# Rounding a quantised layer's weight inside the attention before it, and three tails rearranged in an eight-layer fused kernel

## The reference

```python
x = x + L0_xattn(ln(x), ctx)      # 32 heads of 16, 8 key/value heads
x = x + L0_ffn(ln(x))             # 1792 hidden rows, the winner of each block of 32
x = x + L1_xattn(ln(x), ctx)      # 16 heads of 96, keys from ctx and x
x = x + L1_ffn(ln(x))             # Hadamard rotation, W, bias, LoRA
x = x + L2_xattn(ln(x), ctx)      # 32 heads of 128, 8 key/value heads, normed q and k, mask
x = x + L2_ffn(ln(x))             # fp8: one scale for all of x, one for the weight
x = x + L3_xattn(ln(x), ctx)      # autocorrelation by FFT, top 9 lags, softmax over them
x = x + L3_ffn(ln(x))             # w1, w3, w2 packed as int4 with a scale per group of 64
```

## Time and profile before

| | us |
|---|---|
| median of 3 runs (lowest, highest) | 1610.83 (1609.64, 1613.52) |
| the profiled execution | 1609.08 |
| its span | 1607.4 |
| PE busy | 1400.4 (87%) |
| DVE busy | 1098.7 (68%) |
| ACT busy | 728.5 (45%) |
| POOL busy | 689.5 (43%) |
| mean granted clock of PE | 0.943 of full speed |

### The profile page before, as it was taken

One profiled execution on the slowest core, in us unless ns is written; L12 is line 12 of the kernel. 1 busy time (PEld: TensorE's weight loads), 2 busy tenths in 40 slices (PEclk: granted clock), 3 DMA queues, 4 the chain that ended last, 5 costly groups with the idle time before them and its releaser, 6 DMA issues. The chain is left out here.

```text
span 1607.4 us, 31525 instructions
## 1 busy us (share of the span) xinstructions
PE 1400.4 (87%) x11376; PEld 838.9 (52%) x11376; DVE 1098.7 (68%) x2220; ACT 728.5 (45%) x2379; POOL 689.5 (43%) x662
## 2 busy tenths in 40 slices
PE   5888499986999998669999999999995848659997
PEld 4775244445777776236555655555552325224443
DVE  7997565536657667668878878878776879765212
ACT  4775363213433332228666666666551426354110
POOL 4887441004433334306656666666652025543000
PEclk9998699997999999779999999999998769979998
DMA  7999371109999889346545545665334102276001
GB/s 192 184 172 181 87 158 38 22 6 186 177 181 169 145 136 140 90 124 135 123 109 127 114 113 114 117 138 103 73 76 124 42 0 37 46 155 100 5 1 52
DMA packets 515369, 172.50 MB, mean 107 GB/s; under 512 B 473761, under 2 KB 498657, under 8 KB 515089
## 3 DMA queue, kind: packets, MB, share of 16 engines
q1 hardware_dynamic: 515216, 170.51, 53.6%
HBM read 53.27 MB, written 2.10 MB: 34 GB/s over the span
## 5 line engine op out<-in xcount | busy, mean ns | idle before, releaser
L1714 POOL TENSOR_TENSOR a_q_ss<-a_q_ss,half 128x4 f32<-128x4 f32 x64 | 89.2, 1394 | 188.9 <-DVE a_q_ss L1644 94.9
L1574 ACT ACTIVATE a_probs<-a_masked,a_negmax 128x128 f32<-128x128 f32 x256 | 99.6, 390 | 95.5 <-DVE a_negmax L1619 95.5
L67 PE MATMUL bank<-a_wq_hi,xn_pair 128*128 128x512 f16 (+1 forms) x384 | 139.0, 362 | 0.5 <-DVE a_qn L1649 0.5
L68 PE MATMUL bank<-a_wq_lo,xn_pair 128*128 128x512 f16 (+1 forms) x384 | 138.9, 362 | 0.0
L69 PE MATMUL bank<-a_wq_hi,xn_pair 128*128 128x512 f16 (+1 forms) x384 | 138.7, 361 | 0.0
L1159 POOL TENSOR_TENSOR a_p_hl<-a_probs,a_p_hl 128x512 f16<-128x512 f32 x64 | 74.1, 1158 | 150.0 <-DVE a_p_hl L1097 150.0
L67 PE MATMUL bank<-a_wo_hi,a_o_hi 128*128 128x512 f16 x256 | 97.0, 379 | 6.7 <-DVE x_state L1635 6.7
L69 PE MATMUL bank<-a_wo_hi,a_o_lo 128*128 128x512 f16 x256 | 97.0, 379 | 0.0
L68 PE MATMUL bank<-a_wo_lo,a_o_hi 128*128 128x512 f16 x256 | 97.0, 379 | 0.0
L1616 DVE TENSOR_TENSOR a_masked<-bank,a_mask 128x512 f32<-128x512 f32 x64 | 44.1, 689 | 71.6 <-PE bank L69 71.5
L1729 POOL TENSOR_TENSOR a_normal<-a_probs,a_recip 128x512 f32<-128x512 f32 x64 | 89.8, 1404 | 5.0
(11 more groups left out here) (400 smaller groups left out, 4990.7 us busy)
## 6 DMA issues: line engine op xcount, KB each, us to landing
a_no<-in_L_xattn_Wo SPq DMA_DIRECT2D x9, 1024.0 KB, 5.5
a_nq<-in_L_xattn_Wq SPq DMA_DIRECT2D x8, 1024.0 KB, 5.6
a_n_wq<-in_L_xattn_Wq SPq DMA_DIRECT2D x4, 768.0 KB, 6.6
a_n_wo<-in_L_xattn_Wo SPq DMA_DIRECT2D x4, 768.0 KB, 5.9
a_nk<-in_L_xattn_Wk SPq DMA_DIRECT2D x9, 256.0 KB, 3.1
a_nv<-in_L_xattn_Wv SPq DMA_DIRECT2D x9, 256.0 KB, 2.9
x_state<-in_x SPq DMA_DIRECT2D x8, 256.0 KB, 4.8
a_ctx<-in_ctx_t SPq DMA_DIRECT2D x8, 256.0 KB, 4.0
```

The costliest lines, as they stand in the source:

```text
L67: pe.matmul(out, lh, rh, start=start, stop=False)
L68: pe.matmul(out, lh, rl, start=False, stop=False)
L1574: m = act.activation(probs[s % 2][:, h, :], src, ACT.Exp, bias=negmax[s % 2][:, h:h + 1], accum_out=total[s % 2][:, h:h + 1])
L1714: pool.tensor_tensor(r[:, :], r[:, :], K.half[:, 0:n], ALU.pow).then_inc(root_done.sem, 1)
```

## The change

It has five parts.

1. First attention: ahead items 10 and 11 move from steps 68 and 69 to 75 and 76, behind the last heads; the small weights of stage 1 are loaded at step 50 and split earlier; its first large weights are loaded at step 78, and stage 1, not the end of this one, waits for them.
2. Wide attention: a new class `Quantised` holds the quantised layer's tensors. The weight is loaded at step 6 into half of `xn_rows`, its maximum taken in steps 12 to 15, made common on POOL in step 17, the scale computed in step 18, and the weight rounded in 20 steps of one DVE operation each (20 to 39); ACT casts it in step 61. ctx for the spectra is loaded at step 61. In the tail x of batches 0 to 6 is normalised and its maximum taken, a batch a step.
3. Quantised stage: only batch 7 is normalised; ACT takes the first step of each row's rounding; the 24 spectra are six before the rows and two or three for each batch between them; loops are written out. The packed words of the last layer's tile 0 are loaded here.
4. Lag attention: the ninth largest by one reduction; the sum of weights from the nine values alone; products with a broadcast operand; tile 0 of w1 and w3 is unpacked as chunks 11 and 12; statistics and roots of batches 0 to 3 for the last stage.
5. Last stage: tile 0 needs only its transposes, rows have four buffers, and each batch of x is stored after its own add.

```diff
-    LOAD_FRONT, MEAN_FRONT, CLEAR_FRONT, HIGH_FRONT, LOW_FRONT = TOTAL + 1, TOTAL + 1, TOTAL + 6, TOTAL + 8, TOTAL + 10
-    AHEAD = {B + i: TOTAL + 2 + i for i in range(front.AHEAD)}
+    LOAD_SMALL, MEAN_FRONT, CLEAR_FRONT, HIGH_FRONT, LOW_FRONT, LOAD_FIRST = TOTAL - 14, TOTAL + 1, TOTAL + 2, TOTAL + 3, TOTAL + 10, TOTAL + 14
+    AHEAD = {B: TOTAL + 2, B + 1: TOTAL + 3, B + 2: TOTAL + 11, B + 3: TOTAL + 12}
...
-                    if t == LOAD_FRONT:
-                        front.load(sp, front_small_in, front_first_in)
+                    if t == LOAD_SMALL:
+                        front.load_small(sp, front_small_in)
+                    if t == LOAD_FIRST:
+                        front.load_first(sp)
-                sp.wait_ge(front_first_in, 32)
...
+        self.nw = K.xn_rows[:, KT:2 * KT, :]
+        self.tw, self.te = K.xn_rows[:, 0, :], K.xn_rows[:, 1, :].bitcast(I32)
+        self.wq = K.ctx_hi[:, :, 0:DIM].bitcast(BF16)
...
+        LOAD, LARGEST, SHARED, SCALES, ROUND, CAST, CONTEXT, ROWS = 6, 12, 17, 18, 20, TOTAL - 3, TOTAL - 3, TOTAL - B + ADD
...
+                    if s == LOAD:
+                        sp.wait_ge(norm.ring.filled(B - 1), norm.ring.n_filled(B - 1))
+                        quant.load_weight(sp, quant_in)
+                    if s == CONTEXT:
+                        last = q_last(G - 1)
+                        sp.wait_ge(ring.filled(last), ring.n_filled(last))
+                        quant.load_context(sp, context_in)
+                sp.wait_ge(context_in, 32)
+                    if s == CAST:
+                        for last in (kv_last("k", G - 1), kv_last("v", G - 1)):
+                            act.wait_ge(ring.filled(last), ring.n_filled(last))
+                        act.wait_ge(chain, 1 + 4 + 5 * KT)
+                        act.activation(quant.wq, quant.nw, ACT.Copy).then_inc(cast_done, 1)
...
+                    if part == 0:
+                        link(dve.tensor_scalar(tw, w, quant.scale[:, 0:1], quant.FP8_MAX, ALU.mult, ALU.min))
+                    else:
+                        link(dve.tensor_tensor(w, tw, bits, ALU.subtract))
...
+                    if s == LARGEST:
+                        dve.wait_ge(quant_in, 16)
+                    if LARGEST <= s < LARGEST + KT:
+                        k = s - LARGEST
+                        m = dve.tensor_reduce(quant.weight_max[:, k:k + 1], quant.nw[:, k, :], AX.X, ALU.max, apply_absolute_value=True)
+                    if s == SCALES:
+                        dve.wait_ge(shared_done, 1)
+                        quant.scales(dve, 0, link)
+                    if ROUND <= s < ROUND + 5 * KT:
+                        round_weight(*divmod(s - ROUND, 5))
+                def row_ahead(b):
+                    dve.wait_ge(row_root, 2 * b + 2)
+                    if b == 0:
+                        dve.wait_ge(cast_done, 1)
+                    dve.tensor_scalar(K.xn_rows[:, b, :], K.x[:, b, :], quant.mv[:, b, 0:1], quant.rstd[:, b:b + 1],
+                                      ALU.subtract, ALU.mult).then_inc(row_xn, 1)
+                    dve.wait_ge(row_xn, b + 1)
+                    dve.tensor_reduce(quant.row_max[:, b:b + 1], K.xn_rows[:, b, :], AX.X, ALU.max, apply_absolute_value=True)
...
-                        K.take_stats(dve, b)
+                        r = K.take_stats(dve, b)
+                        if b < quant.ahead:
+                            link(r)
+                            dve.bn_aggr(quant.mv[:, b, :], K.stats[:, b, :]).then_inc(row_mean, 1)
...
+                def row_root_of(b):
+                    pool.wait_ge(row_mean, b + 1)
+                    pool.tensor_scalar(quant.rstd[:, b:b + 1], quant.mv[:, b:b + 1, 1], EPS, None, ALU.add).then_inc(row_root, 1)
+                    pool.wait_ge(row_root, 2 * b + 1)
+                    pool.tensor_tensor(quant.rstd[:, b:b + 1], quant.rstd[:, b:b + 1], K.half[:, 0:1], ALU.pow).then_inc(row_root, 1)
...
+                    if s == SHARED:
+                        pool.wait_ge(largest_done, 1)
+                        pool.partition_all_reduce(quant.whole[:, 0:1], quant.big[:, 0:1], P, bass.bass_isa.ReduceOp.max).then_inc(shared_done, 1)
+                    if 0 <= s - ROWS < quant.ahead:
+                        row_root_of(s - ROWS)
...
+            if q == 0:
+                engine.wait_ge(front.first_in, 32)
...
+    EARLY = 6
+    LATER = {i: list(range(EARLY + 3 * i, EARLY + 3 * i + 3)) if i < 2 else list(range(EARLY + 2 + 2 * i, EARLY + 4 + 2 * i)) for i in range(B)}
...
-                sp.dma_start(nw[:, :, :], weight.rearrange("(k p) n -> p k n", p=P)).then_inc(inw, 16)
                 packed.load_down(sp, words_here)
-                sp.wait_ge(words_here, 32)
+                packed.load_first(sp, words_here)
...
+                def round_fp8(b):
+                    dve.wait_ge(scaled_done.sem, scaled_done.count(b))
+                    link(dve.tensor_scalar(e[:, :], w[:, :].bitcast(I32), 0x7F800000, None, ALU.bitwise_and))
+                    link(dve.tensor_scalar(bits, bits, 2.0 ** -6, Q.MAGIC, ALU.max, ALU.mult))
+                    link(dve.scalar_tensor_tensor(w[:, :], w[:, :], -Q.FP8_MAX, bits, ALU.max, ALU.add))
+                    if b >= 2:
+                        dve.wait_ge(t_bank.filled(b - 2), t_bank.n_filled(b - 2))
+                    dve.scalar_tensor_tensor(xq[b % 2][:, :], w[:, :], Q.TOP, bits, ALU.min, ALU.subtract).then_inc(q_done.sem, 1)
...
+                dve.bn_aggr(Q.mv[:, LAST, :], K.stats[:, LAST, :]).then_inc(row_mean, 1)
+                dve.wait_ge(row_root, 2)
+                link(dve.tensor_scalar(xn[:, LAST, :], K.x[:, LAST, :], Q.mv[:, LAST, 0:1], Q.rstd[:, LAST:B], ALU.subtract, ALU.mult))
+                link(dve.tensor_reduce(Q.row_max[:, LAST:B], xn[:, LAST, :], AX.X, ALU.max, apply_absolute_value=True))
+                dve.tensor_reduce(Q.big[:, 1:2], Q.row_max[:, :], AX.X, ALU.max).then_inc(largest_done, 1)
                 dve.wait_ge(whole_done, 1)
...
+                Q.scales(dve, 1, link)
+                dve.sem_inc(scale_done, 1)
+                link(dve.tensor_tensor(Q.out_by[:, :], Q.back[:, 0:1], Q.back[:, 1:2], ALU.mult))
+                for b in batches:
+                    round_fp8(b)
+                    if b >= 2:
+                        add(b - 2)
+                add(B - 2)
+                add(B - 1)
...
-                spectra.multiply(pe)
+                spectra.begin(pe)
+                for u in range(EARLY):
+                    spectra.multiply(pe, u)
                 pe.wait_ge(const_done, 2)
...
+                    for u in LATER[b][0:1]:
+                        spectra.multiply(pe, u)
...
+                    for u in LATER[b][1:]:
+                        spectra.multiply(pe, u)
...
-                spectra.copy(act)
+                def scale(b):
+                    if b >= 3:
+                        act.wait_ge(q_done.sem, q_done.count(b - 3))
+                    act.activation(tw[b % 3][:, :], xn[:, b, :], ACT.Copy, scale=Q.scale[:, 1:2]).then_inc(scaled_done.sem, 1)
+                for u in range(EARLY):
+                    spectra.copy(act, u)
+                act.wait_ge(scale_done, 1)
+                for b in range(2):
+                    scale(b)
...
+                    if b + 2 < B:
+                        scale(b + 2)
+                    for u in LATER[b]:
+                        spectra.copy(act, u)
...
-        UNPACK = {-2: (0, 1, 2), -1: (3, 4, 5, 6), 0: (7, 8), 1: (9, 10)}
+        UNPACK = {-2: (0, 1, 2), -1: (3, 4, 5, 6), 0: (7, 8), 1: (9, 10), B: (11, 12)}
...
-                            act.wait_ge(own.sem, own.count("total", l))
+                            act.wait_ge(own.sem, own.count("left8", l))
+                    if m is not None:
+                        act.wait_ge(own.sem, own.count("beyond", m))
+                        act.activation(nine_e[:, :, :], beyond[:, :, :], ACT.Exp).then_inc(nine_done.sem, 1)
...
-                        for k in range(KT):
-                            i = dve.max(next8[:, k, :], left8[:, k, :])
-                        i.then_inc(own.sem, 1)
+                        dve.tensor_reduce(next8[:, :, 0], left8[:, :, :], AX.X, ALU.max).then_inc(own.sem, 1)
-                        dve.memset(next8[:, :, 1:8], GONE).then_inc(own.sem, 1)
-                        dve.wait_ge(own.sem, own.count("alone", m))
-                        dve.memset(spacer[:, :], 0.0)
+                        if m:
+                            dve.wait_ge(nine_done.sem, nine_done.count("x", m - 1))
+                        dve.tensor_tensor(beyond[:, :, :], nine[:, :, 0:9], nine[:, :, 0:1].broadcast_to([P, KT, 9]),
+                                          ALU.subtract).then_inc(own.sem, 1)
...
-                        dve.wait_ge(own.sem, own.count("picked", m))
-                        dve.tensor_reduce(total[:, :], picked[:, :, :], AX.X, ALU.add).then_inc(own.sem, 1)
```

(71 more changed lines are left out.)

337 lines of the change are left out of this document (191 added, 146 removed).

## The result

The changed kernel takes 1590.32 us (median of 4 runs, 1587.60 to 1594.24) against 1610.24 of the kernel before (median of 4): a ratio of 0.9875, 95% interval 0.9849 to 0.9900. That is 20 us faster where 38 were forecast, and 2.3 us above the upper end of the range (1560 to 1588). The profiled execution's span is 1588.7 us against 1607.4, so 18.7 of the difference can be followed in the traces.

A forecast was written before the change was run, and what follows sets the result against it. PE was taken to bound the wide attention, DVE the lag attention, with the quantised stage poorly overlapped. Terms -9.6 + 2.0 + 2.0 - 14.5 - 4.3 - 8.0 - 5.6 = -38.0 us gave 1573 us from 1610.83; range 1560 to 1588.

The forecast's parts named there:

- The sum's largest term: Quantised stage: work leaves the path to the first row and PE sets the loop; 14.5 us gained, range 8 to 18.
- Rival (2): Quantised loop: PE stays at the low clock, +21 us, 1594; 8%.
- The all-reduce: Wide attention, step 17: POOL's stall of 5.6 us behind the call costs PE 2.0 us; bounds nothing and 8.
- Rival (1): Step 17: the code load is paid before the all-reduce too, 6 us more POOL stall, +6, 1579; 12%.
- The lag attention: Lag attention: DVE's step 0.94 us shorter, less the added work; 4.3 us gained, range 2 to 6.
- small subtraction: Lag attention step: one reduction of 0.69 us and this subtraction replace four maxima, memset and gaps, saving 0.25 us.
- The last stage's start: Last stage: PE starts at about 10.9 us, second tile at 21.5; 8 us gained, range 5 to 10.5.
- The first attention's tail: End of first attention: last heads cast straight behind the mix; 9.6 us gained, between 5 and 12.
- Rival (3): First attention's tail: the last heads don't come earlier, only the forecast's 9.6 us goes, 1583; 12%.
- The wide attention's tail: Steps 61 to 68: the ACT cast and DVE's rows ahead cost 2.0 us, range 1 to 5.
- Stores: End of kernel: the last 256 KB goes out right behind its add; 5.6 us gained, range 5 to 6.5.
- Rival (5): Wide attention: DVE's added step makes it late for PE in each of 28 steps, +56 us, 1629; 3%.

The follow-up runs named there:

- e14: Changed kernel with the rows of all eight batches normalised at the head of the quantised stage, none in the wide attention's tail: 1585.92 us (0.9862).
- e1: Changed kernel with the all-reduce of the wide attention's step 17 replaced by a POOL copy of 128 x 1 values: 1582.07 us (0.9829).
- e5: Changed kernel with chunks 11 and 12 unpacked in step 2 of the lag attention instead of step 8: 1586.67 us (0.9857).
- e9: Changed kernel with stage 1's first large weights loaded four steps earlier, at step 74: 1588.94 us (0.9863).
- e10: Changed kernel with ahead items 10 and 11 back at steps 68 and 69, loads as changed: 1592.13 us (0.9887).
- e13: Changed kernel with all four loads for stage 1 back at step 65, ahead items 10 and 11 still behind the last heads: 1588.46 us (0.9883).

## Why the prediction was wrong, point by point

**The sum's largest term held.** The quantised stage gave 14.5 of 14.5. Its working (six spectra and their copies, then ACT's scaling and DVE's steps, 16.9 us to the first row; 3.1 a batch, PE in front) was met within 0.3 us and in its order: the copies ended 13.4 us into the stage, forecast 13.9. Rival (2), the low clock, did not come: transposes take 0.39 in the loop (its sum is 48.4 us and not 48.6, which changes nothing). The cover of 9 us for the all-reduce held too, with half a microsecond to spare, against a stall that the forecast didn't have; that was luck. What was wrong is that rows made in the tail were counted among what the head gains. With the copies in front they gave it nothing (e14), and the tail paid for them.

**The all-reduce (+9.6 instead of +2.0)** is the term that sank the forecast. The step that failed is the use of the earlier trace rows: the call begins 0.23 us after its input "since POOL had been idle 12.26 us", and from this I charged step 17 with the stall behind the call alone, though POOL has no such idle time there. The stall on the way in runs from the end of POOL's last ordinary operation, whether the input is there or not: 5.6 to 6.0 us in the twelve traces with a call in the wide attention, 8.8 to 9.8 in the quantised stage behind such a call, 6.75 without one (e1). In e14 the call is prompt behind 8.33 us of idle time, and in the earlier trace rows behind 12.26. That row could not tell "no stall" from "a stall that is hidden". The stall behind the call was short as well, 7.68 against 5.6. In the earlier trace rows the 5.6 are what is left behind the root's input; from the first DVE operation of the lag attention to the root it is 7.1 us there, and 6.9 in the changed kernel. With both stalls the root of step 18 is 11.5 us late, where I had 5.6. And the forecast had no term for the clock: of the 9.6 us PE stood idle for 7.75 and lost the other 1.9 at 1.2 GHz behind it. The range's upper bound for the term, 8, was 1.6 too low.
Rival (1) was this case at 12%, with a price of 6 on top of the 2.0: right in its mechanism, and 1.6 short, since the stall behind the call and the clock were not in it. The Trainium skill's rule (GPSIMD Engine Reference, 2.1 Instruction dispatch: about 6 us before the first call to a freshly loaded kernel, nothing shown for it) agrees with the 5.6 to 6.0 of the first call, not with the 8.8 to 9.8 of the next one; the stall on the way out is in the trace alone.

**The lag attention (+2.2 instead of -4.3)** had two mis-sized terms. The six steps gave 3.0 (from -8.69 to -11.74 at the same instruction), 0.5 each, where 0.94 was forecast: from the end of the first replacement to the start of the second it was to be 0.25 shorter and is 0.33 longer, since the "small subtraction", 0.20 with POOL idle, takes 0.75. The two chunks were to take 1.0 and took 5.06. Both kinds are DVE operations on SBUF that run beside POOL's; I priced them from rows in which POOL was idle, and had the earlier trace rows for the place alone. e5 moved the chunks to an idle POOL and they took their 0.28 each. The Trainium skill has the rule (SBUF — State Buffer, Who interferes with whom): a cast or a tensor_scalar on SBUF can take the port pair that DVE shares with GpSimd, and the one that comes second stands for the whole instruction of the other; a DVE operation with two inputs in SBUF contends with one of GpSimd that reads there. The trace agrees: 0.43 alone and 1.26 beside POOL for the same cast in the last stage, 0.28 against 1.12 to 1.35, 0.20 against 0.60 to 0.75, while operations with one input in a bank keep their 0.69.

**The last stage's start (-5.2 instead of -8.0).** PE starts 12.6 us in, not 10.9. SP's two transposes of the first weights, 3.5 us, stood before the rows' and were not in the sum; that DVE and POOL took 7.5 us for the rows, not 5.7 (the cast beside POOL again), did not matter behind them. But the late start costs little, since PE waits again anyway. Its second wait ends 22.1 us in, forecast 21.5, and the term that was missing is what comes behind it: PE has been idle for 2.84 us and takes eight matmuls at 1.2 GHz, one every 0.43 us instead of 0.22, 1.7 us in all. The forecast gave the slow matmuls to the first tile alone. The second wait's end (0.6), this clock (1.7) and the rounding from 7.7 to 8 make 2.6 of the 2.8. In other traces of the same stage the loss is between 0.8 and 3.1.

**The first attention's tail (-7.5 instead of -9.6).** The last add and its statistics end at 172.8 (171.0 to 173.2 over the ten traces), forecast 169.5. The last mix ends at 158.6 instead of 156, and the add of batch 6, which frees the bank, is done at 166.8 instead of 163: it comes behind a low part for which DVE had waited 2.18 us for ACT's cast, and behind an ahead row. ACT's wait for the first weights was 2.3 us instead of 1.5, but it can't be seen at the next joint (e9). The cause was half wrong: each of the two edits does it alone (e10, e13), so the move of the items, priced at 9.6 in the forecast, gives little once the loads are moved: the last add is at 171.91 without it, and at 169.6 to 171.8 with it. Rival (3) did not come.

**The wide attention's tail (+3.1 instead of +2.0).** PE waits 1.50 and 0.55 for a_o_lo, since a row ahead stands in front of it on DVE in steps without 1.4 us of idle time. The run without these rows (e14) has 2.8 us of it back. **Stores (-6.5 instead of -5.6):** right; the span ends 2.4 us behind the last add and not 3.2. **Rival (5)** did not come: steps 20 to 39 with a rounding step each take 7.84 us on average, a few 8.8 to 9.1 with the lost time back in the next.

The range failed since it let one price be wrong at a time. The two largest misses, 14 of some 19 us, have one origin: the all-reduce and DVE's small operations were priced from places where POOL was idle.

## What to carry to other kernels

An all-reduce on POOL costs a stall on the way in and another on the way out, here 6 to 10 and about 7 us, once for two calls in a row; a row in which it is prompt shows only that POOL was idle for long before. Idle time ahead of the call hides the first stall. It did not hide the second, which stood ahead of the next ordinary operation even after 41 us without one. Where neither is covered, make the maximum common with a matmul and a reduction (1.5 us here). And price a DVE operation on SBUF by a row with POOL at work if POOL will be at work: the same operation took three to nearly five times as long.
Before work is moved off a path, ask what would then end that path. Here two other things ended it at nearly the same time, POOL's stall and ACT's copies, so the move gained nothing there and cost what it cost elsewhere.

## What the runs showed of the hardware

- POOL's stall ahead of an all-reduce was 5.6 to 6.0 us in the wide attention (twelve traces), 8.8 to 9.8 in the quantised stage behind it (ten), and 6.75 there when the earlier call was gone (e1). Behind the call in the wide attention it was 6.7 to 7.7. At the head of the lag attention POOL's first root begins 5.2 us behind its input (1287.43 and 1292.62), 6.9 behind the stage's first DVE operation. Why the lengths differ was not tried.
- The spread of a version over four runs was 3.3 to 7.9 us with the call in the wide attention (1587.60 to 1594.24 for the changed one) and 2.0 to 3.6 without any call. The stalls do not explain it: both together vary by 1.2 us over the twelve traces, while the first masked scores of the wide attention, ahead of any call, vary by 5.3 over ten. What varies there was not tried.
- Behind a wait of 7.75 us, and behind one of 2.84, PE's matmuls of 512 columns followed each other every 0.43 us (1.2 GHz) instead of 0.22 (2.4 GHz), which cost 1.9 and 1.7 us.
- Four transposing DMAs in a row are issued in 5.4 to 5.6 us in every trace of the last stage. The two ahead of them, behind ordinary loads, take 3.2 to 4.95 in the same order of the program.
